# Three edits in one kernel: a new order in layer 1's front, one factor matmul per chunk and diagonal products in layer 3

## The reference, cut to what matters

```python
# layer 1, per batch of 512 rows xn = layernorm(x)
score = (xn @ Wq) @ (xn @ Wk).T / sqrt(32)    # causal; zeros become a large negative number
a     = softmax(score) @ (xn @ (Wvdown @ Wvup))
y     = max(softmax(xn @ router_w + router_b)) * (xn @ expert_w[argmax] + expert_b[argmax])
# layer 3 attention: chunks of 64 rows, a state M of 128 x 128 per batch
outputs  = chunk @ M.T
v_target = mean(silu(outputs @ vg_w1.T) @ vg_w2.T + outputs)      # mean over the chunk's 64 rows
M        = decayed M + rate * (v_target - M k_mean) k_mean.T,  scaled by its norm
a        = silu(outs @ vg_w1.T) @ vg_w2.T + outs                  # over all 512 rows, at the end
# layer 3 experts: 2 of 8 per row, and a shared one
y        = shared(xn) + w1 * expert_i1(xn) + w2 * expert_i2(xn)
```

## Time and profile before

| | |
|---|---|
| median of 3 runs | 1391.28 us (1389.5 to 1394.29) |
| the profiled execution: its time / its span | 1392.78 us / 1391.0 us |
| busy: PE, PEld, DVE, ACT, POOL | 83%, 58%, 72%, 55%, 44% of the span |
| layer 1's work | about 575 to 723 us |
| layer 3's work | about 1194 to 1391 us |
| the span's mean granted TensorE clock | 0.922 of full speed |

### The profile page before, as it was taken

The page is one execution under the profiler, slowest core; times in us unless marked ns, Lnnn a source line. Parts: engine busy times, 40 slices in busy tenths (PEclk is TensorE's granted clock), DMA queues, the critical chain, the costliest instruction groups (busy, mean ns, idle before and its releaser), DMA issues. The chain is left out here.

```text
span 1391.0 us, 21029 instructions
## 1 busy us (share of the span) xinstructions
PE 1151.0 (83%) x7010; PEld 811.3 (58%) x7010; DVE 999.5 (72%) x2280; ACT 763.7 (55%) x1586; POOL 614.8 (44%) x607
## 2 busy tenths in 40 slices
PE   3999999999898879367766888888888977889995
PEld 1455665665465568156653655655645655668885
DVE  2466767678787727277765989989998999535555
ACT  1456556555544527144446867667768675345552
POOL 4243445444336834554100533733643565216672
PEclk9999999999999989589987999999899889799997
DMA  7400000000000023550000000000000000101113
GB/s 176 121 1 1 1 1 1 1 1 1 1 5 22 28 63 116 154 163 16 1 13 0 1 1 1 1 1 1 1 1 1 1 1 0 31 10 40 43 44 107
DMA packets 54443, 40.71 MB, mean 29 GB/s; under 512 B 13185, under 2 KB 46687, under 8 KB 54337
## 3 DMA queue, kind: packets, MB, share of 16 engines
q1 hardware_dynamic: 40994, 27.58, 6.8%
q0 software_dynamic: 4544, 9.32, 2.4%
q10 hardware_dynamic: 8800, 2.48, 0.9%
HBM read 26.32 MB, written 13.04 MB: 28 GB/s over the span
## 5 line engine op out<-in xcount | busy, mean ns | idle before, releaser
L780 POOL TENSOR_TENSOR PR<-PR,R 128x512 f32<-128x512 f32 (+3 forms) x128 | 160.3, 1264 | 233.1 <-DVE R L1275 232.5
L1985 POOL TENSOR_TENSOR YY<-YY,H 128x512 f32<-128x512 f32 x120 | 164.1, 1390 | 182.0 <-DVE H L2438 182.0
L410 PE MATMUL banks<-XT,we 128*128 128x128 f32 (+1 forms) x568 | 175.8, 442 | 14.0 <-ACT HH L2258 13.7
L1074 ACT ACTIVATE PR<-banks,NM 128x257 f32<-128x257 f32 (+3 forms) x256 | 132.2, 526 | 94.7 <-DVE NM L1247 93.0
L410 PEld LDWEIGHTS banks<-we,HH 128*128 128x128 f32 x1024 | 144.9, 205 | 35.7 <-issue 31.2
L2430 DVE TENSOR_TENSOR_SCAN H<-wide,H 128x1024 f32<-128x1024 f32 x64 | 164.1, 2564 | 0.2
L410 PE MATMUL banks<-we,HH 128*128 128x128 f32 x1024 | 145.1, 288 | 0.0
L410 PEld LDWEIGHTS banks<-XT,we 128*128 128x128 f32 x568 | 89.5, 201 | 65.5 <-issue 41.2
L2258 ACT ACTIVATE HH<-banks,be1f 128x512 f32<-128x512 f32 x128 | 83.4, 685 | 73.7 <-PE banks L410 72.8
L410 PE MATMUL banks<-BCR,SEL 96*128 96x512 f32 x128 | 67.1, 526 | 63.8 <-DVE H L2438 55.4
L410 PEld LDWEIGHTS banks<-PTS,V 128*64 128x64 f32 x1152 | 65.7, 138 | 83.4 <-issue 48.5
(11 more groups left out here) (568 smaller groups left out, 2445.9 us busy)
## 6 DMA issues: line engine op xcount, KB each, us to landing
xsort<-zrow SPq DMA_DIRECT2D x1, 3072.0 KB, 13.6
XS<-xsort SPq DMA_DIRECT2D x12, 256.0 KB, 2.9
ysort<-PTS SPq DMA_DIRECT2D x12, 256.0 KB, 2.2
pj_stage<-in_L_ffn_w_proj SPq DMA_DIRECT2D x1, 2048.0 KB, 11.9
we<-in_L_ffn_we SPq DMA_DIRECT2D x1, 2048.0 KB, 15.3
we<-yrows SPq DMA_DIRECT2D x8, 256.0 KB, 5.4
xrows<-XN SPq DMA_DIRECT2D x4, 256.0 KB, 3.4
out<-XN SPq DMA_DIRECT2D x4, 256.0 KB, 2.3
```

Source lines behind the costliest of these rows:

```text
L410: return nc.tensor.matmul(o, l, r, start=start, stop=stop)
L780: last = nc.gpsimd.tensor_tensor(p, p, R[:, T * q + t, :].unsqueeze(2).to_broadcast([P, 2, w]), ALU.mult)
L1074: nc.scalar.activation(PR0[:, q % 2, s, OFF[t]:OFF[t] + w], ps2(n)[:, s, SLOT[t]:SLOT[t] + w], ACT.Exp, bias=NM[:, m, s:s + 1], accum_out= ...
L1985: nc.gpsimd.tensor_tensor(YY[:, m, :], YY[:, m, :] if n else XD[m], H[:, k % 4, m, :], ALU.add).then_inc(ya, 1)
```

## The change

In layer 1:

- The 18 turned blocks are spread over all five iterations, six in the first. There TensorE turns them after all its other steps of the iteration, ahead of `features(1)`, and ACT stores one between `exps(0, 1)` and `exps(0, 2)`, one before `exps(0, 3)` and four after `gate_next(1)`. The other iterations turn three each, and no block stands between experts 5, 6 and 7 any more.
- On ACT `exps(j, 2)` and `exps(j, 3)` come before `store_s(b, 2)` and `store_s(b, 3)`.
- On DVE `choose(j)` comes after `apply_in(j + 1)`, and `add_expert(b, 6)` therefore directly after `stats_in`; `add_expert(b, 0)` waits on the semaphore of `choose`.

In layer 3:

- `HAZ` holds the four batches' columns of a chunk side by side, so that one matmul takes the place of four.
- `final(b)` uses banks 4 to 7, one per batch, and waits for no store; `SA3` and its stores on ACT are gone, and `gate_and_add` reads the bank.
- DVE no longer combines. It makes 32 diagonal matrices `DG` (the identity times the weights, eight operations of 128x512). TensorE adds `ACC` in banks 0 to 3 by 16 products with the identity, and then 32 products of a diagonal with the rows in `YB`. ACT takes the silu from the bank.

The diff, cut to its core:

```diff
-                TURNS = [(), range(0, 4), range(4, 8), range(8, 12), range(12, 18)]
+                TURNS = [range(0, 6), range(6, 9), range(9, 12), range(12, 15), range(15, 18)]
 # layer 1, TensorE
                                 expert(b, 5)
-                                turn(TURNS[j][3:4])
                                 expert(b, 6)
-                                turn(TURNS[j][4:])
                                 expert(b, 7)
+                            else:
+                                turn(TURNS[0])
 # layer 1, ScalarE
                             if front:
                                 exps(j, 1)
+                            if not back:
+                                store_turned(TURNS[0][0:1])
+                            if front:
+                                exps(j, 2)
+                            if not back:
+                                store_turned(TURNS[0][1:2])
+                            if front:
+                                exps(j, 3)
                             if back:
                                 store_s(b, 2)
                                 store_s(b, 3)
-                                store_turned(TURNS[j][3:4])
-                            if front:
-                                exps(j, 2)
-                                exps(j, 3)
                             if more:
                                 gate_next(j + 1)
                             if back:
-                                store_turned(TURNS[j][4:])
                                 gate(b)
+                            else:
+                                store_turned(TURNS[0][2:])
 # layer 1, VectorE
                                 inverse(b)
+                                v.wait_ge(wgs, b + 1)
                                 add_expert(b, 0)
...
                                 stats_in(j + 1)
-                            if front:
-                                choose(j)
                             if back:
                                 add_expert(b, 6)
                             if more:
                                 apply_in(j + 1)
+                            if front:
+                                choose(j)
                             if back:
                                 add_expert(b, 7)
 # layer 3
-                HAZ = sbr("HAZ", [P, NM * NM], c=c)
+                HAZ = sbr("HAZ", [P, NC, NM], c=c)
+                DG = fcT[:, 0:E, :].rearrange("p e (i q) -> p (e i) q", q=P).rearrange("p (k m) q -> p k m q", k=2)
 # TensorE
                         def final(b):
                             pe.wait_ge(hs, NC)
-                            if b >= 2:
-                                pe.wait_ge(fos, b - 1)
                             for t in range(T):
-                                o = PS[:, 6 + b % 2, t * P:(t + 1) * P]
+                                o = PS[:, 4 + b, t * P:(t + 1) * P]
...
                                 pe.wait_ge(ha, k + 1)
-                                for b in range(B):
-                                    m = b * NC + k
-                                    last = mm(PS[0:NM, 7, 0:P], HAZ[:, m * NM:(m + 1) * NM], vg2m[:, :], start=False, stop=b == B - 1)
-                                last.then_inc(er, 1)
+                                mm(PS[0:NM, 7, 0:P], HAZ[:, k, :], vg2m[:, :], start=False, stop=True).then_inc(er, 1)
...
                         for b in range(B):
                             final(b)
+                        pe.wait_ge(ac, B - SH)
+                        pe.wait_ge(re_, NS)
+                        pe.wait_ge(oe, NS)
+                        for b in range(B):
+                            for t in range(T):
+                                mm(PS[:, b, t * P:(t + 1) * P], ident[:, :], ACC[:, b, t, :], start=t == 0, stop=False)
+                        for b in range(B):
+                            pe.wait_ge(dg, b + 1)
+                            pe.wait_ge(yl[b], 32)
+                            for t in range(T):
+                                for k in range(2):
+                                    last = mm(PS[:, b, t * P:(t + 1) * P], DG[:, k, b * T + t, :], YB[:, b, k, t, :], start=False,
+                                              stop=t == T - 1 and k == 1)
+                            last.then_inc(ad, 1)
 # ScalarE
                         for b in range(B):
-                            act.wait_ge(fo, b + 1)
                             if b >= 2:
                                 act.wait_ge(done, b - 1)
-                            nc.scalar.activation(SA3[:, b % 2, :, :].rearrange(flat), PS[:, 6 + b % 2, :], ACT.Copy).then_inc(fos, 1)
                             act.wait_ge(ad, b + 1)
-                            nc.scalar.activation(GS[:, b % 2, :, :], ACC[:, b, :, :], ACT.Silu).then_inc(gt, 1)
+                            nc.scalar.activation(GS[:, b % 2, :, :].rearrange(flat), PS[:, b, :], ACT.Silu).then_inc(gt, 1)
 # VectorE: combine() and gate_out() go, and in their place
+                        v.wait_ge(wf, NS)
+                        for b in range(B):
+                            for k in range(2):
+                                last = nc.vector.tensor_tensor(DG[:, k, b * T:(b + 1) * T, :],
+                                                               ident[:, :].unsqueeze(1).to_broadcast([P, T, P]),
+                                                               WK3[:, k, b * T:(b + 1) * T].unsqueeze(2).to_broadcast([P, T, P]),
+                                                               ALU.mult)
+                            last.then_inc(dg, 1)
+                        for b in range(B):
                             v.wait_ge(gt, b + 1)
-                            v.wait_ge(fos, b + 1)
-                            gate_and_add(link, GS[:, b % 2, :, :], SA3[:, b % 2, :, :], X4[:, b, :, :],
-                                         XN4[:, b, :, :]).then_inc(done, 1)
+                            v.wait_ge(fo, b + 1)
+                            gate_and_add(link, GS[:, b % 2, :, :], PS[:, 4 + b, :].rearrange("p (t d) -> p t d", t=T),
+                                         X4[:, b, :, :], XN4[:, b, :, :]).then_inc(done, 1)
```

More of the change, by code:

```diff
@@ L2607, in layer3 @@
             nq, nn, nrm, srt = (lsem(f"a3_{k}") for k in ("squares", "norm_sum", "norm_stored", "norm_root"))
-            fo, fos, done = (lsem(f"a3_{k}") for k in ("final", "final_stored", "output"))
+            fo, done, dg = (lsem(f"a3_{k}") for k in ("final", "output", "diagonals"))
             shifted, expd = lsem("f3_shifted"), lsem("f3_expd")
@@ L2674, in layer3 @@
                 NR = sbr("NR", [P, NC, B], c=c)
-                SA3 = sbr("SA3", [P, 2, T, D], c=c)
                 GS = sbr("GS3", [P, 2, T, D], c=c)
@@ L2739, in _ @@
                         nc.gpsimd.tensor_tensor(NSQ[:, :], NSQ[:, :], half16[:, :], ALU.pow).then_inc(ns, 1)
-                        nc.gpsimd.memset(HAZ[:, :], 0.0).then_inc(zeroed, 1)
+                        nc.gpsimd.memset(HAZ[:, :, :], 0.0).then_inc(zeroed, 1)
                         nc.gpsimd.tensor_copy(N[:, :, :], M0T[:, :].unsqueeze(1).to_broadcast([P, B, P])).then_inc(zeroed, 1)
@@ L3175, in _ @@
                                     v.wait_ge(zeroed, 4)
-                                nc.vector.reduce_sum(HAZ[:, (NM + 1) * k:(NM + 1) * (k + (B - 1) * NC) + 1:(NM + 1) * NC],
+                                nc.vector.reduce_sum(HAZ[:, k, k:k + (B - 1) * NC + 1:NC],
                                                      HS[:, :, k * CH:(k + 1) * CH], AX.X).then_inc(ha, 1)
```

17 lines of the change are left out of this document (removed).

## The result

The changed kernel takes 1379.11 us (median of 6 runs, 1376.52 to 1381.58), the kernel before 1390.2 (6 runs, 1388.27 to 1394.29): a ratio of 0.9914, with a 95% interval of 0.9897 to 0.9931. The profiled execution took 1379.6 us.

A forecast was written before the change was run, and what follows sets the result against it. No engine is always busy; the costs lie at layer 1's iteration boundaries, layer 3's chunks and its end. Gains of 7.5 + 4.7 + 2.4 = 14.6 us from 1391.3 give 1376.7 us, range 1372 to 1383.

The forecast's parts named there:

- clock behind the queries: Rival: layer 1's inner boundaries give nothing, as the low clock moves behind the queries; 1381.5 us, chance 0.15.
- First boundary: Layer 1 after iteration 0: 0.5 us from earlier rows and delayed silu, 1.0 from the clock; together 1.5 (-0.3 to 3.0).
- Inner boundaries: Layer 1 after iterations 1 and 2: VectorE's idle time goes, queries start 1.9 us earlier each, 3.8 together.
- signs of being wrong: TensorE waiting in the end, GpSimd never idle in the chunks, or a clock near 0.5 behind the stored features.
- Boundary after iteration 3 and iteration 4: End of layer 1: expert 0 starts 0.5 us earlier, the last sum 1.7 earlier; together 2.2 (1.7 to 2.7).
- Layer 1 in all: Sum of layer 1's boundary gains: 7.5 us (1.4 to 10.5).
- Chunks: Layer 3: six of eight factor matmul records go in each of seven chunks, 0.67 us each, 4.7 us (to 5.2).
- another chain bounds the chunks: Rival: GpSimd or another chain bounds layer 3's chunks, so their 4.7 us are not gained; 1381.4 us, chance 0.05.
- The end: Layer 3's end: TensorE does 160 records without a wait, and the last sum ends 2.4 us earlier.
- Scatter held: Rival: VectorE's eight diagonals block GpSimd's last scatter by up to 5.5 us; 1380.0 us, chance 0.05.
- The end at 1.2 GHz: Rival: layer 3's end runs at the low clock, its 160 records adding 17.9 us; 1394.6 us, chance 0.03.
- the clock back everywhere: Rival: TensorE's clock returns, putting layer 1 at its upper bounds, some 10 us; 1374.0 us, chance 0.12.

The follow-up runs named there:

- turns_only: Kernel before with the turned blocks spread and ScalarE's new order, without the choice's move: 1384.11 us against 1391.59, one run.
- gap_split_again: gap_split's kernel unchanged, measured on another occasion: 1374.26 us, ratio 0.9872 to the kernel before.
- factor_only: Kernel before with only layer 3's `HAZ` side by side and one matmul per chunk: 1387.53 us, ratio 0.997.
- late_diag: Changed kernel, but VectorE waits for the last scatter's landing before writing the diagonals: 1381.35 us, one run.
- gap_split: Changed kernel with gap_turns' and split_tail's edits together: 1376.72 us, ratio 0.9906 to the kernel before.
- gap_turns: Changed kernel with three turned blocks of each of iterations 1 and 2 moved to the iteration's end, stored ahead of `gate`: 1378.4 us, ratio 0.9908.
- choice_only: Kernel before with only the choice of the expert moved behind the normalized rows, and its wait: 1393.55 us against 1391.42, one run.
- clock_fill: Changed kernel with 24 unused transposes on TensorE in iterations 2 and 3, ahead of features and queries: 1381.94 us, ratio 0.9937.
- split_tail: Changed kernel with batch 0 of layer 3's combination on VectorE, only batches 1 to 3 on TensorE: 1379.12 us, ratio 0.992.

## Why the prediction was right

The time was forecast at 1376.7 us and is 1379.1, within the range and inside the forecast's own 1374.5 to 1379.5. Part of that is luck: the gain was forecast at 14.6 us and is 11.1 from median to median, 3.5 less, and 1.1 of this is hidden by a starting time that was too high (1391.3 from three runs, 1390.2 from six). By the time alone the rival "clock behind the queries" (1381.5) is as near as the forecast; the trace tells them apart. By its steps:

- **First boundary**, forecast 1.5: 1.85. The silu came 0.20 later, as said; a turned block took 1.8 us in the pause and not 1.3, still just in time; and the rows L396 0.54 earlier (0.5); the other 1.3 is the clock (1.0), with the queries at 1.02 us instead of 1.83. But the blocks in the long pause, from which the forecast had it, don't give it alone: turns_only has them and loses 0.12. The right size is in part luck.
- **Inner boundaries**, forecast 1.9 each: 2.22 and 0.51. VectorE's part came as worked out (no idle time ahead of L473, the rows 3.7 us earlier), and so did the queries' start, 1.85 and 1.92 us earlier against the row L482 before them. What failed is the size at one of the two: the rival "the clock behind the queries" came true there and not at the other, and with it one of the signs of being wrong, a clock near 0.5 behind the stored features (0.60 in the window from 672.00). I gave this rival 0.15 and took it for all or nothing. In the five traces with the changed kernel's layer 1 (or with only the stores moved) that I compared, iteration 3 has it every time (33.73 to 34.15). turns_only shows besides that the choice's move, costed as part of this gain, takes from it there: the last sum, which holds up the stored features, is 1.9 us earlier against L482 with ScalarE's part alone, and 1.2 with the choice's move added.
- **Boundary after iteration 3 and iteration 4**, forecast 2.2: 2.75, nearly the same in every trace without blocks between the last experts but gap_split_again's. The last three sums now follow each other without a pause and take 3.58 us from the first start to the last end, where it was 5.15: 1.6, forecast 1.7. The other 1.2 was forecast as 0.5 and put down to the choice's move; turns_only has it in full without that move.
- Layer 1 in all: 7.35 against 7.5, of which the misses at the inner boundaries (-1.1) and the surplus elsewhere (+0.9) cancel, by luck.
- **Chunks**, forecast 4.7: 4.76, with 0.66 in chunk 0 as in the others, and GpSimd's idle time 0.81 against the forecast 0.8; factor_only alone gives 4.58, so the rival "another chain bounds the chunks" is out. Not foreseen: 0.41 lost ahead of the first chunk, a cost of the smaller `HAZ` that the prediction put at nothing.
- **The end**, forecast 2.4: 2.32 in the trace, by the mechanism as told (160 records at a clock of 1.00, the end 20.17 after the first record, forecast 20.1). But against other traces of the old tail it is 1.4 to 2.3: the one profiled execution flattered it.
- **Scatter held**: it was forecast as nothing or as 5.5 us, and is 0.46, with no effect on the end. The Trainium skill, page "SBUF — State Buffer", section "Who interferes with whom", says that a VectorE instruction with two SBUF inputs contends with a GpSimd instruction that reads SBUF, and calls the port pair they share an exclusive lock; that the other engine is fully blocked for the whole instruction it writes of VectorE's two-port modes. late_diag bears out that there is contention, but 0.46 us is less than one diagonal operation's 0.6 (4.90 for the row of eight) and far from all of them.
- **The end at 1.2 GHz** and **the clock back everywhere** did not come: the clock is 1.00 in the end, and 0.60 behind the second boundary's stored features.
- **Layer 2**, not in the sum: +0.66. It is 470.32 to 470.39 in the four traces in which layer 1 is as before or has the turns alone, 470.96 to 471.16 in seven with more, but 470.16 and 470.49 in the two of gap_split, whose layers 1 and 2 are gap_turns' (471.03). No line of layer 2 differs. Windows over the whole of layer 2, of gap_turns and then of gap_split:

```profile
715.36:1186.39 471.03, 383.50 (x1748) 258.58 (x1749) 420.69 (x630) 321.49 (x454) 210.70 (x176) 0.90 0.00 2
```

```profile
712.34:1182.50 470.16, 380.23 (x1748) 257.37 (x1749) 420.41 (x630) 321.44 (x454) 210.55 (x176) 0.91 0.01 2
```

The counts are equal on all engines, VectorE, ScalarE and GpSimd are busy for the same time within 0.3 us, and TensorE for 3.27 less at a slightly higher clock. So most of it is where TensorE's low stretches fall. That the edits shift them through the time at which layer 1 ends was not tested, and choice_only's 472.49 stays unexplained.

The trace's sum is 13.14 and the time's is 11.1 from median to median. The rest lies in the runs: before's profiled execution was 2.6 above the median of its six runs, the changed kernel's 0.5 above.

## What to carry to other kernels

Where TensorE's clock is low behind a pause, as at these boundaries, put work that nobody waits for behind the pause, and don't count on filler to remove the low stretch: in clock_fill it only pushed it onto the work that matters. A step that comes earlier gains nothing if what the next one waits for hangs on another chain, as the rows L396 did. Add up removed work at the engine that is never idle in that stretch (the chunks and the end came within 0.1 us in the trace), and price a move that only reorders an engine with the other edits in place, because choice_only and turns_only together promise 8.9 us where 7.35 came. Compare stages over several traces before a gain of one or two microseconds is believed: the old tail alone varied by 0.9.

## What the runs showed of the hardware

- The same instructions can take 137.64 or 141.85 us in layer 1 (gap_split twice), by where TensorE's clock is at 0.50. Layer 3 up to the first `HAZ` was 55.63 us in one trace and 58.42 to 59.61 in all others. In that trace (split_tail) the clock was already partly back in a stretch in which the changed kernel had 0.50 throughout; their windows, from 15 us after the first statistics of layer 3 on, split_tail first:

```profile
1199.90:1204.90 5.00, 5.00 (x36) 5.00 (x35) 4.03 (x16) 0.00 (x0) 0.00 (x0) 0.76 0.00 0
```

```profile
1203.00:1208.00 5.00, 5.00 (x26) 5.00 (x25) 3.85 (x15) 0.00 (x0) 0.00 (x0) 0.50 0.00 0
```

- Layer 1's first statistics start anywhere between 572.66 and 577.82 us, ahead of any edited line's effect; single executions are therefore no measure for differences of a few microseconds.
- An indirect scatter on GpSimd takes 1.43 or 1.44 us instead of 0.97 when six or eight 128x512 products of VectorE from SBUF operands start beside it (eight traces), and is not held for all of them.
- Shorter work off the critical path can cost time through TensorE's clock: `HAZ` zeroed in 0.31 and not 0.95 us left one row of TensorE at 5.47 instead of 3.84 us, and the first chunk 0.43 later (factor_only).
